# A gated attention block on one core: orders written out to the fourth pair of tiles, split probabilities turned one pair later, squares of six tiles summed by ScalarE

## The reference

```python
def reference(x, ctx_4096, g_xattn, g_ffn, weight_real, bias):      # names shortened
    # x: 4 x 1024 x 2048, ctx: 4 x 64 x 2048, weight: 2048 x 2048
    q = layernorm(x)
    a = einsum('bqd,bkd->bqk', q, ctx)
    c = einsum('bqk,bkd->bqd', softmax(a), ctx)
    x = x + tanh(g_xattn[0]) * c
    W = mean(abs(weight_real), axis=1, keepdims=True) * sign(weight_real)
    x = x + tanh(g_ffn[0]) * (einsum('bsi,oi->bso', layernorm(x), W) + bias)
    return x
```

## Time and profile before

| | before |
|---|---|
| median of 3 runs | 1012.34 us (1010.96 to 1014.2) |
| the profiled execution | 1012.6 us |
| its span, first to last instruction | 1010.8 us |
| its mean granted TensorE clock | 0.981 |

### The profile page before, as it was taken

The page is one execution under the profiler, slowest core; times in us unless marked ns, Lnnn a source line. Parts: engine busy times, 40 slices in busy tenths (PEclk is TensorE's granted clock), DMA queues, the critical chain, the costliest instruction groups (busy, mean ns, idle before and its releaser), DMA issues.

```text
span 1010.8 us, 14224 instructions
## 1 busy us (share of the span) xinstructions
PE 941.6 (93%) x5201; PEld 464.3 (46%) x5201; DVE 870.4 (86%) x1213; ACT 563.7 (56%) x617; POOL 149.8 (15%) x268
## 2 busy tenths in 40 slices
PE   2659999899999799999999899999999899999998
PEld 2435554444444344444444444444444444444443
DVE  6788999799989989897989989898989989897834
ACT  5999851545567574735557473735567473742310
POOL 0111022301112120202011120302011120302000
PEclk9779999899999899999999999999999999999999
DMA  9879718657887989796796988687797869674552
GB/s 311 270 223 240 205 22 219 178 104 170 171 198 172 226 167 227 132 201 170 164 217 121 242 172 214 143 195 173 157 215 137 239 120 214 157 162 102 112 125 83
DMA packets 365140, 178.66 MB, mean 177 GB/s; under 512 B 353424, under 2 KB 353424, under 8 KB 354448
## 3 DMA queue, kind: packets, MB, share of 16 engines
q1 hardware_dynamic: 365072, 177.76, 74.9%
HBM read 55.58 MB, written 33.55 MB: 88 GB/s over the span
## 4 chain that ended last, share of the span: by engine, by line
PE 56%; issue 17%; DVE 16%; POOL 4%; ACT 3%; DMA 2%; SPq 0%; POOLq 0%; ACTq 0%; DVEq 0%
PE y_ps L1930 46%; PE s_ps L1862 4%; PE c_ps L1878 4%; DVE natural L1157 3%; PE y_ps L1898 2%; DVE xr L1233 2%; DMA xr<-in_x_dram 2%; DVE xr L1365 2%; ACT xn_q L763 1%; DVE snap_a L1275 1%; DVE xr L1278 1%; DVE snap_a L1272 1%; DVE st L1236 1%; POOL nm L631 1%; POOL ve L639 1%
## 5 line engine op out<-in xcount | busy, mean ns | idle before, releaser
L1930 PE MATMUL y_ps<-wsign,ring_a 128*128 128x512 fp8e4 x1792 | 407.0, 380 | 0.0
L1930 PEld LDWEIGHTS y_ps<-wsign,ring_a 128*128 128x128 f16 x1792 | 174.4, 98 | 208.5 <-issue 2.1
L1930 PE MATMUL y_ps<-spare,ring_a 128*128 128x512 fp8e4 x896 | 198.9, 379 | 0.7 <-ACT snap_b L880 0.7
L1930 PEld LDWEIGHTS y_ps<-spare,ring_a 128*128 128x128 f16 x896 | 86.9, 98 | 105.3 <-ACT snap_b L880 1.7
L1233 DVE SCALAR_TENSOR_TENSOR xr<-c_ps,coef,xr 128x512 f32<-128x512 f32 x128 | 95.5, 746 | 26.0 <-PE c_ps L1878 25.6
L763 ACT ACTIVATE xn_q<-xr,nm,r 128x1024 f32<-128x1024 f32 x62 | 76.9, 1241 | 56.8 <-DVE natural L1157 35.4
L747 ACT ACTIVATE natural<-xn_a 128x1024 f16<-128x1024 f32 x76 | 79.2, 1053 | 44.7 <-DVE xn_a L1378 34.6
L1930 PE MATMUL y_ps<-sg,ring_a 128*128 128x512 fp8e4 x448 | 99.4, 379 | 0.0
L1157 DVE TENSOR_TENSOR natural<-xn_a,natural 128x1024 f16<-128x1024 f32 x78 | 94.7, 1216 | 4.7 <-ACT natural L747 4.7
L1878 PE MATMUL c_ps<-kd,pt 128*128 128x512 f16 x256 | 80.7, 398 | 13.8 <-DVE xr L1233 10.9
L1236 DVE BATCH_NORM_STATS2 st<-xr 128x6 f32<-128x512 f32 x128 | 88.9, 694 | 4.4
(11 more groups left out here) (116 smaller groups left out, 1012.3 us busy)
## 6 DMA issues: line engine op xcount, KB each, us to landing
xr<-in_x_dram SPq DMA_DIRECT2D x32, 1024.0 KB, 5.9
out_dram<-xr SPq DMA_DIRECT2D x30, 1024.0 KB, 4.6
spare<-n_L_ffn_weight_real_dram SPq DMA_DIRECT2D x8, 1024.0 KB, 6.1
ctx_f<-in_ctx_dram SPq DMA_DIRECT2D x8, 512.0 KB, 7.3
xr<-n_L_ffn_weight_real_dram SPq DMA_DIRECT2D x4, 1024.0 KB, 7.4
ctx_f<-n_L_ffn_weight_real_dram SPq DMA_DIRECT2D x4, 1024.0 KB, 6.8
out_dram<-xr SPq DMA_DIRECT2D x8, 256.0 KB, 2.2
ring_a<-natural SPq DMA_TRANSPOSE x102, 4.4
```

Of the source, the lines that this page charges most:

```text
L1930: last = nc.tensor.matmul(y_ps[:, BANKS[j] + n, :], ring_a[:, slot_a(p, j), part, k, :], RIGHT[j][:, k // 2, chunk(n), k % 2], start=(firs ...
```

## The change

- **Written out to the fourth pair.** All engines' lists are written out for pairs 0 to 3 and the loop starts at pair 4; the lists of the start, of the pairs and of the three loop variants are written in another order, and the tables with them.
- **Turned probabilities of the second tile.** `transpose_probs(f + 1)` and `copy_pt(f + 1)` move from the end of a pair into the next, behind two half products (in the pair after a key change it already stood so for the tile before).
- **Squares by ScalarE.** For tiles 4 to 9 (`LN2_ACT`) the addition in `attention` also hands out the sum of what it writes, and the four `bn_stats` and the `bn_aggr` go; `square_rows2(u)` on ScalarE makes the mean from the four sums and sums the squares in one pass; `scale2(u)` has three further one-column operations and not four. `junk`, where the pass writes, lies in `xn_q`, so query rows and passes wait for each other.
- **Other loads.** All 16 weight sums go to ScalarE (`ABS_DVE` is empty), tile 2's first sums too (`DVE_LN1` 3 to 2).

```diff
-    ABS_DVE = (2, 5, 8, 11, 14)
+    ABS_DVE = ()
...
-        DVE_LN1 = 3
+        DVE_LN1 = 2
+
+
+        LN2_ACT = range(4,10)
+
+        def sums_by(engine_is_act, u):
+            return sum(1 for v in range(u) if (v in LN2_ACT) == engine_is_act)
...
             def scale2(u):
-                pool.wait_ge(mv2_set, u + 1)
+                if u in LN2_ACT:
+                    pool.wait_ge(sq2_set, sums_by(True, u) + 1)
+                    nc.gpsimd.tensor_scalar(ve2[:, :], sq2[:, :], X1_SCALE ** -2 / D, EPS * X1_SCALE ** -2, ALU.mult,
+                                            ALU.add).then_inc(ve2_set, 1)
+                    finish_scale2(u)
+                    nc.gpsimd.tensor_tensor(nm2[:, :], mean2[:, u % 2:u % 2 + 1], r2[:, :], ALU.mult).then_inc(nm2_set, 1)
+                    return
...
             def square_rows1(u):
                 act.wait_ge(mean1_set, u - DVE_LN1 + 1)
                 if u > DVE_LN1:
                     act.wait_ge(ve1_set, u)
+                if squared:
+                    act.wait_ge(sq2_set, len(squared))
...
+            def square_rows2(u):
+                v, m = sums_by(True, u), slice(u % 2, u % 2 + 1)
+                act.wait_ge(x1_set, (u + 1) * NC)
+                if v > 0:
+                    act.wait_ge(mean2_set, v)
+                if v > 1:
+                    act.wait_ge(nm2_set, u - 1)
+                nc.scalar.activation(scaled2[:, :], sum2[:, u % 2, :], ACT.Copy, scale=-1.0 / D,
+                                     accum_out=mean2[:, m]).then_inc(mean2_set, 1)
+                act.wait_ge(mean2_set, v + 1)
...
+                nc.scalar.activation(junk, xr[:, u % RX, :], ACT.Square, bias=mean2[:, m],
+                                     accum_out=sq2[:, :]).then_inc(sq2_set, 1)
...
             sign(4)
+            sum_rows1(2)
+            copy_pt(0)
             take_w(0)
-            copy_pt(0)
-            sign(4)
+            square_rows1(2)
...
+                if u in LN2_ACT:
+                    v = sums_by(True, u)
+                    if n == 0 and v > 1:
+                        dve.wait_ge(mean2_set, v - 1)
+                    nc.vector.scalar_tensor_tensor(out=xr[:, r, chunk(n)], in0=c_ps[:, :],
+                                                   scalar=coef[:, u % 2:u % 2 + 1], in1=xr[:, r, chunk(n)], op0=ALU.mult,
+                                                   op1=ALU.add, accum_out=sum2[:, u % 2, n:n + 1]).then_inc(x1_set, 1)
+                    return
...
-            for p in range(2, PAIRS_N):
+            for p in range(4, PAIRS_N):
                 f = PLAIN + 2 * (p + 2)
...
                     half_product(p, 0, 0, 0)
                     half_product(p, 0, 0, 1)
                     if more:
+                        transpose_probs(f - 1)
+                    half_product(p, 0, 1, 0)
+                    if more:
                         attend(f - 2, 1)
...
+                    half_product(p, 6, 0, 0)
                     if later:
                         transpose_probs(f)
-                    half_product(p, 6, 0, 0)
-                    if later:
-                        scores(f + 1)
                     half_product(p, 6, 0, 1)
                     half_product(p, 6, 1, 0)
                     half_product(p, 6, 1, 1)
                     if later:
-                        transpose_probs(f + 1)
+                        scores(f + 1)
```

More of the change, by code:

```diff
@@ L2145, in _ @@
+            half_product(3, 5, 1, 0)
+            half_product(3, 5, 1, 1)
+            half_product(3, 6, 0, 0)
+            half_product(3, 6, 0, 1)
+            half_product(3, 6, 1, 0)
+            half_product(3, 6, 1, 1)
+            transpose_probs(14)
+            scores(15)
+            for p in range(4, PAIRS_N):
                 f = PLAIN + 2 * (p + 2)
@@ L2268, in _ @@
                     half_product(p, 5, 0, 0)
+                    if later:
+                        scores(f)
                     half_product(p, 5, 0, 1)
```

1221 lines of the change are left out of this document (742 added, 479 removed), and 16 rows, old and new, of the table NAT.

## The result

The change made the kernel slower: the median is 1025.0 us (1023.41 to 1029.17) against 1012.34 us, five runs of each, a ratio of 1.0125 with a 95% interval of 1.0106 to 1.0144. The forecast was 994 us, the range 984 to 1007. The profiled execution of after took 1029.17 us, span 1027.3 us, at a mean clock of 0.973; it is the slowest of its five runs, 4 us over their median, which has to be kept in mind when spans are subtracted.

What follows compares the result with a forecast made beforehand. TensorE sets the pace where others keep up; elsewhere VectorE's order of work decides. 1012.6 - 26.8 (Set A, Set B, Set C) + 3 (new waits) + 5 (hand-overs) = 993.8 us, range 984 to 1007.

Steps and rivals of the forecast that it cites:

- Set C: Pair loop around a change of keys: TensorE waits of 1.03, 0.47 and 3.45 us, twice, all 9.9 us to go.
- The hand-over of a plain pair: Query-row halves side by side on VectorE wait for ScalarE: 2.5 us lost per key period, 5 us; upper end 12.8.
- What bounds the kernel: TensorE sets the pace where others keep up; elsewhere VectorE's order of work decides; only TensorE's waits and slow clock winnable.
- VectorE's load: 32.6 us less work on VectorE before about 270 us; no gain by itself, but lets Set A and Set B go.
- Set A: Tile 5's attention: TensorE's waits of 3.15 and 1.13 us and 2.42 us of slower products go, 6.7 us.
- Set B: End of the second pair: waits for probabilities of tiles 10 and 11 and slower products behind go, 10.2 us.
- New waits in the first pairs: Orders written out to the fourth pair bring new waits: 3 us taken, bounds none and 10.2 us.
- GpSimd is held: Rival, tiles 5 to 8: weight differences delay GpSimd's row statistics, 12.6 us in place of 3, 1003.4 us; chance 0.17.
- slower: Rival: VectorE's handovers become the loop's period, 3.9 us a pair if uncovered, 1020 us; chance 0.08.
- Second output of an addition: 24 attention updates on VectorE also write a sum: 0.1 us each, 2.4 us; upper end 6.3 us.
- The start-up: Before the first column blocks: ScalarE's added passes stay hidden with 1.4 us left; nothing counted, 3 us either way.
- What would show it: Right: probability waits below 10 us, attention-update waits below 5, third pair some 15 us earlier; wrong: plain pairs 57 us or more.

Runs made afterwards that it cites:

- experiment 6: Changed kernel with two 4.4 us weight combinations moved to later places on VectorE in the first pair, loop untouched: 1025.96 us, 1.0111 of before.
- experiment 8: Kernel before, with the last tile's probabilities turned and copied in the next pair for pairs 5 and 9: 1013.73 us, 1.0002 of before.
- experiment 9: experiment 5 plus four more moves, in the first pair, at the end of pair 3 and around the key change: 1007.49 us, 0.9944 of before.
- experiment 14: experiment 5 with second statistics of tiles 4 to 9 and five weight sums back on VectorE: 1014.08 us, 1.0012 of before.
- experiment 5: Changed kernel with three loop moves: VectorE work between query-row halves, key-maximum reduction after tile f + 1's statistics, key-change snapshot ahead of normalise2: 1007.76 us, 0.9943 of before.
- experiment 3: Changed kernel with GpSimd's key-maximum reduction moved behind the mean and deviation of tile f + 1: 1024.56 us, 1.0098 of before.
- experiment 10: Changed kernel with ScalarE's first snapshot ahead of normalise2(f - 1) in the key-change pairs 4 and 8: 1024.49 us, 1.011 of before.
- experiment 13: experiment 5 with three VectorE weight combinations beside the first pair cut to a quarter of their elements, the rest left out: 1000.6 us, 0.9879 of before.
- experiment 2: Changed kernel with two finish_pair calls moved between the halves of low query rows on VectorE in plain pairs: 1021.27 us, 1.0074 of before.
- experiment 12: Changed kernel with the second tile's probabilities turned and copied at the pair's end again, in every loop variant: 1051.91 us, 1.0372 of before.

## Why the prediction was wrong

The forecast was 1012.6 - 26.8 + 3 + 5 = 993.8 us; the profiled execution took 1029.17, 35.4 us more. From the start to pair 4 the miss is 13.9 - 1.2 = 12.7 us, from there on 17.7 + 4.9 = 22.6 us; 4 us of the whole are this execution's distance from the median. By terms, the loop's 22.6 us are 13.3 of Set C, some 6 of a reduction that was not priced and some 3 of the hand-over.

- **What bounds the kernel: wrong in its use.** It said that the order in which VectorE comes to its work decides, and then counted each wait that an instruction no longer stood in as won. Experiments 6, 8 and 9 show that such waits reappear, in part or in full, at the next instruction that needs VectorE. This is the step behind the failures in the first pairs and in Set C.
- **VectorE's load**, not a gain by itself but what lets A and B go: borne out by experiment 14, where the order without it is as fast as before.
- **Set A** was right in place: pair 0 begins 3.7 us earlier, where 3.15 + 2.42 = 5.6 us were due by then, and the rows have no answer in after, where TensorE runs 120 products in 26.06 us from 180.12 us on. **Set B** went as well; tile 11's probabilities cost nothing.
- **New waits in the first pairs**, 3 us with 10.2 as the upper end: mis-sized. They are 3.14 + 2.94 us in the first pair, 0.91 + 0.43 + 0.50 + 3.34 us in pair 3, 11.3 us in all. And the slow clock behind them, which Set A had counted, was put at nothing here: it fell behind three of them. Pair 0 lasts 66.5 us in after and 62.4 in experiment 5, with the same instructions and waits, so 4.1 us of it are clock. With the 8.3 us of waits beyond the 3 that is 12.4 of the 12.7 us. Two of them are the rival "GpSimd is held", with a chance of 0.17; its mechanism was there, at 3.88 and 4.11 us, but experiment 6, where GpSimd is free, loses as much at VectorE's combinations themselves. The Trainium skill, "SBUF — State Buffer", section "SBUF: two separate sides", says that a VectorE operation with two inputs in that memory and a GpSimd operation that reads it exclude each other for a whole instruction. The trace agrees again: GpSimd's columns end with VectorE's combinations, at 207.89 and 207.84 us.
- **Set C**, "All 9.9 us lose their cause": wrong, and the largest miss of the loop, 9.9 + 3.4 = 13.3 us (2.9 of them the clock behind pair 3's last wait). Pairs 8 and 9 take 116.2 us (807.29 - 691.11) after 116.8 (795.00 - 678.23), pairs 4 and 5 even 120.7 after 116.8. The three waits were replaced by 2.41, 0.81 and 1.07 us at other places. Experiment 8 made one of the moves in the old kernel and won nothing.
- **The hand-over of a plain pair**, 2.5 us for each key period with 12.8 us at the upper end: mis-sized, by less than Set C. Pairs 6, 10 and 11 lose 5.7 us and pair 7, by an estimate from these, some 2 of its 8.4, so about 8 us where 5 were taken. The count of idle was right in kind (2.3 us twice, and the bias behind), and its measure close: 2.60, 1.90 and 0.69 us, 5.2 for 4.8. The cover was wrong. 50.00 + 4.8 left 0.7 us, but VectorE also stands 0.31 + 0.68 us in the attention, has 1.27 us in short gaps and 0.29 us more work, so a plain pair is over by 2.26 us (57.74 - 55.48) and not under by 0.7. The rival "slower" named this mechanism with 3.9 us a pair and a chance of 0.08.
- **Not priced at all:** the reduction of the key maximum ahead of a mean on GpSimd (4.62 us and a slower clock, some 6 us of pair 7; experiment 3), and ScalarE's snapshot behind `normalise2` (2.41 us twice, experiment 10; part of Set C's miss). Both are moves in the diff that the prediction doesn't mention; the trace of before has no wait there.
- **Second output of an addition**, taken at 0.1 us: 24 rows of 82 ns (DVE_READ_ACCUMULATOR), 2.0 us. Right. The Trainium skill, "VectorE: DVE Perf Modes", section "Two Vector instructions with no wait between them", calls it a second instruction, and the trace lists it as one.
- **The start-up**, nothing with 3 us either way: right within these bounds. Of the 5.6 us that Set A was to bring by pair 0, 3.7 came, so some 1.9 us were lost ahead of it.
- **What would show it**: the list named idle of VectorE in the loop with TensorE waiting for a result behind a query row, and pairs of 57 us or more. That is what the profile shows. None of the signs of being right came: the waits are 15.4 us and not under 10, 5.6 and not under 5, and the third pair begins 6.4 us earlier and not 15.

What stays open: how much of the first pairs' bound is VectorE's own time and how much its hold on GpSimd (experiment 13 lessens both), and how the 6.3 us of experiment 14 divide between the squares, the sums and the clock.

## What to carry to other kernels

In a list that is written by hand a wait is a symptom of an engine's lateness: before counting it as won, find the next instruction that needs the same engine and see whether that one would wait instead. Two halves that pass through one buffer don't stand side by side on the engine that reads them; put other work of the length of the refill between them, as the two moved calls of experiment 2 did. And of each moved call on a small engine ask what stands behind it there: the three moves of experiment 5 turned 1.25% slower into 0.6% faster. Last, try the order and the shifted work apart: here the order, even with the three moves, was by itself worth nothing (experiment 14).

## What the runs showed of the hardware

The same wait costs TensorE its clock in one execution and not in another. In six runs (of after and experiments 10, 3, 2, 5 and 12) the instructions are the same up to about 376 us, with the same waits of 3.1 and 2.9 us. In the profiled execution of after the 8 products behind the first took 3.62 us (above); in experiment 5, TensorE's timeline:

```profile
215.53 0.23 PE L2112 MATMUL s_ps<-ident,prob 128*128 128x128 f16 x1 [3.15 <-DVE prob L1390]
215.60 1.89 PE L2173 MATMUL y_ps<-wsign,ring_a 128*128 128x512 fp8e4 x8
```

Over these 8 products the granted clock is 1.00 in experiment 5 and 0.50 in after: 1.89 us is 2.4 GHz, 3.62 us is 1.2 GHz. Over 205 to 370 us the granted clock was 0.97, 0.97, 0.98, 0.98, 1.00 and 1.00 in these six, and the same half product in pair 3 began at 376.0, 375.7, 374.6, 374.3, 371.1 and 370.6 us. Pair 0, which has both waits, lasts 66.5, 66.5, 65.3, 65.2, 62.4 and 62.4 us in the same order. So some 4 of the 5.4 us of spread lie behind two waits near 3 us, the rest ahead of pair 0, and single moves of that size (experiments 3 and 10) can't be told by the total; the traces tell them.
